# Four buffers instead of two for sorted tokens and overflow rows, and another place for the overflow units' work, in a two-expert feed-forward kernel on one Trainium2 core

## What is computed

```python
# x: (2, 2048, 512), so 4096 tokens of 512 numbers; cond: (2, 512)
ys = cond / sqrt(512)
d  = rsqrt(einsum('bi,io->bo', ys*ys, wc*wc) + 1e-8)
xf = (einsum('bsi,io->bso', x * ys[:, None, :], wc) * d[:, None, :]).reshape(4096, 512)
top1 = argmax(softmax(xf @ gate_w.T))            # one of 2 experts per token
masked = xf[None] * one_hot(top1).T[:, :, None]  # a token is zero for the other expert
h = relu(einsum('end,edh->enh', masked, w1) + b1[:, None, :])      # hidden size 2048
routing = (einsum('enh,ehd->end', h, w2) + b2[:, None, :]).sum(axis=0)
shared = relu(xf @ sw1 + sb1) @ sw2 + sb2
out = x + (routing + shared).reshape(2, 2048, 512)
```

## Time and profile before

| | |
|---|---|
| median of 3 runs | 1457.22 us (1457.13 to 1457.71) |
| the profiled execution's own time | 1471.43 us |
| its span, first to last instruction | 1469.7 us |
| mean granted clock of PE, share of full | 0.975 |
| PE busy | 1390.4 us |
| DVE, ACT, POOL busy | 904.7, 642.5, 282.6 us |
| moved by DMA | 317.65 MB, mean 216 GB/s |

### The profile page before, as it was taken

One profiled execution on the slowest core, in us unless ns is written; L12 is line 12 of the kernel. 1 busy time (PEld: TensorE's weight loads), 2 busy tenths in 40 slices (PEclk: granted clock), 3 DMA queues, 4 the chain that ended last, 5 costly groups with the idle time before them and its releaser, 6 DMA issues.

```text
span 1469.7 us, 17093 instructions
## 1 busy us (share of the span) xinstructions
PE 1390.4 (95%) x6086; PEld 1146.9 (78%) x6086; DVE 904.7 (62%) x1313; ACT 642.5 (44%) x929; POOL 282.6 (19%) x260
## 2 busy tenths in 40 slices
PE   9999999998899657999899999999999999999995
PEld 8888888887688445788788888888888887888884
DVE  7979978584796321867357787877784443333331
ACT  4455645453466332566567444444553221222220
POOL 0000006322222232200000000001001222055665
PEclk9999999999999878899999999999999999999998
DMA  6957584977998446773357797979898756366653
GB/s 211 311 181 243 193 265 163 262 249 268 302 303 258 158 155 191 258 205 109 125 187 257 247 291 247 285 249 310 289 277 297 200 148 155 90 187 165 165 128 59
DMA packets 223925, 317.65 MB, mean 216 GB/s; under 512 B 51440, under 2 KB 98544, under 8 KB 223824
## 3 DMA queue, kind: packets, MB, share of 16 engines
q1 hardware_dynamic: 200528, 267.06, 55.9%
q0 software_dynamic: 22016, 47.00, 12.9%
q10 hardware_dynamic: 1296, 2.49, 0.5%
HBM read 184.47 MB, written 140.90 MB: 221 GB/s over the span
## 4 chain that ended last, share of the span: by engine, by line
PE 84%; DMA 6%; issue 4%; POOL 2%; DVE 2%; ACT 1%; SPq 0%; ACTq 0%; POOLq 0%; DVEq 0%
PE bank L1852 38%; PE bank L1922 21%; PE bank L1951 18%; PE bank L1780 6%; DMA loose_rows<-x_rows,tab_in 3%; POOL loose_rows L847 1%; POOL out L833 1%; DMA hidden_scratch<-vb 1%; DMA rows<-sorted_scratch 1%; DMA sorted_scratch<-sorted_rows 1%; PE bank L1875 1%; DVE rows L1331 0%; DMA hidden_scratch<-vt 0%; DVE vb L1400 0%; DMA loose_rows<-loose_rows,loose_at 0%
## 5 line engine op out<-in xcount | busy, mean ns | idle before, releaser
L1852 PE MATMUL bank<-xw,w_hi 128*128 128x512 f32 x1792 | 561.3, 395 | 58.1 <-ACT vb L990 36.5
L1852 PEld LDWEIGHTS bank<-xw,w_hi 128*128 128x128 f32 x1792 | 340.8, 191 | 132.6 <-issue 34.5
L1367 DVE TENSOR_TENSOR hl<-hin,hl 128x512 fp32r<-128x512 f32 x352 | 236.5, 688 | 264.1 <-ACT hl L966 263.3
L966 ACT CAST hl<-hin 128x512 fp32r<-128x512 f32 x352 | 216.7, 621 | 385.1 <-PE bank L1951 223.6
L1852 PE MATMUL bank<-xw,w_lo 128*128 128x512 f32 x896 | 352.7, 394 | 0.0
L1951 PE MATMUL bank<-w_hi,hl 128*128 128x512 f32 x1024 | 315.9, 390 | 1.3 <-DVE res_u L1702 1.3
L1922 PE MATMUL bank<-hl,w_hi 128*128 128x512 f32 x896 | 276.0, 390 | 0.0
L1951 PEld LDWEIGHTS bank<-w_hi,hl 128*128 128x128 f32 x1024 | 192.3, 188 | 41.5 <-issue 1.7
L1951 PE MATMUL bank<-w_lo,hl 128*128 128x512 f32 x512 | 199.4, 390 | 0.0
L1852 PEld LDWEIGHTS bank<-xw,w_lo 128*128 128x128 f32 x896 | 170.8, 191 | 35.8
L1922 PEld LDWEIGHTS bank<-hl,w_hi 128*128 128x128 f32 x896 | 168.3, 188 | 34.8
(11 more groups left out here) (184 smaller groups left out, 1197.0 us busy)
## 6 DMA issues: line engine op xcount, KB each, us to landing
hin<-hidden_scratch SPq DMA_DIRECT2D x112, 512.0 KB, 4.6
hidden_scratch<-vb SPq DMA_DIRECT2D x80, 512.0 KB, 4.2
hin<-expert_hidden SPq DMA_DIRECT2D x64, 512.0 KB, 4.5
expert_hidden<-vb SPq DMA_DIRECT2D x48, 512.0 KB, 3.8
hidden_scratch<-vt SPq DMA_DIRECT2D x32, 512.0 KB, 4.4
w_new<-w_shared SPq DMA_DIRECT2D x52, 256.0 KB, 5.9
sorted_scratch<-sorted_rows POOLq DMA_DIRECT2D x48, 256.0 KB, 4.4
ring<-x_cols SPq DMA_DIRECT2D x32, 256.0 KB, 5.1
```

The lines of the kernel that those rows point to most:

```text
L966: nc.scalar.copy(hl[:, n % HL, 0, :], hin[:, n // 2 % LOADS, n % 2, :]).then_inc(hu_hi, 1)
L1367: nc.vector.tensor_tensor(hl[:, n % HL, 1, :], hin[:, n // 2 % LOADS, n % 2, :], hl[:, n % HL, 0, :].bitcast(F32), ALU.subtract).then_inc( ...
L1852: last = nc.tensor.matmul(up_bank(u, UP_BANK[c])[p][:], w[:, DOWN_W[c], pair, part], xw[:, c, x, k, :], start=(c in FRESH and n == 1), sto ...
```

## The change

Five things change.

1. `sorted_rows` has four buffers (at 208, 210, 212 and 214 KB), and POOL's loop stores tile k-2 after it has issued the gather of tile k. A gather waits for the store of tile k-4. The fourth buffer lies beyond the plan's 215 KB on tile `soft`, which is allocated right behind the plan now; `rows_u` is a view of `soft`. So ACT at the start of group 20 waits for all 48 tiles.
2. `loose_rows` has four buffers too, with the semaphores of the sort. The order of POOL's steps in the output stage stays.
3. `loose_up` uses banks 4 to 7 for products and 2 and 3 for transposes, and waits at first only for the sums of c = 3. The first transposes stand between the third and the fourth group of products; ACT's work is in the same order, and its loads of the next rows stand behind the relus. PE's last wait for all relus is gone.
4. `loose_down` runs before slot j = 8 of unit 3, uses a bank of unit 2, and PE does not wait for `loose_sum` behind it. ACT's and DVE's parts move by eight slots.
5. PE waits for `loose_down_done` before unit 4.

```diff
-LOOSE_DOWN = 3
+LOOSE_DOWN = (3, 8)
...
-        sorted_rows = [at(kb, f"sorted_rows{i}", [D]) for i, kb in enumerate((208, 210))]
+        sorted_rows = [at(kb, f"sorted_rows{i}", [D]) for i, kb in enumerate((208, 210, 212, 214))]
...
-        loose_rows = [at(kb, f"loose_rows{i}", [D]) for i, kb in enumerate((164, 166))]
+        loose_rows = [at(kb, f"loose_rows{i}", [D]) for i, kb in enumerate((164, 166, 200, 202))]
...
-        loose_banks, loose_turned = banks[0:QUADS], banks[QUADS:QUADS + 2]
+        loose_banks, loose_turned = banks[QUADS:2 * QUADS], banks[2:4]
...
             def sort_in(k):
+                i, u = k % RING, SORT[k]
                 pool.wait_ge(up_mm, PER_GROUP * SORT_GROUP + 2 * k)
-                wait(pool, sorted_out[k % 2], DMA * (k // 2))
+                wait(pool, sorted_out[i], DMA * (k // RING))
...
-            for k in range(COLS):
-                sort_in(k)
-                if k > 0:
-                    sort_out(k - 1)
-            sort_out(COLS - 1)
+            for k in range(COLS + 2):
+                if k < COLS:
+                    sort_in(k)
+                if k >= 2:
+                    sort_out(k - 2)
...
                     if u == LOOSE_UP[0] and not spilled:
-                        for i in range(2):
-                            act.wait_ge(sorted_out[i], DMA * ((SORT.index(COLS - 1) + 1) // 2))
+                        for i in range(RING):
+                            act.wait_ge(sorted_out[i], DMA * COLS // RING)
...
+                pe.wait_ge(loose_lo, 2 * x + 2)
+                pe.wait_ge(up_added, 6 * u + 2)
+                for q in range(QUADS - 1):
+                    products(q)
+                pe.wait_ge(up_added, 6 * (u + 1))
+                turn_back(0)
+                products(QUADS - 1)
+                for q in range(1, QUADS):
+                    turn_back(q)
-                pe.wait_ge(loose_relu, HC * (x + 1))
...
-                pe.wait_ge(loose_sum, 2 * x + 2)
...
+                if wide == LOOSE_DOWN[0] + 1:
+                    pe.wait_ge(loose_down_done, 2)
```

More of the change, by code:

```diff
@@ L318, in build @@
         b2_in = sem("b2_in")
-        sorted_in = [sem(f"sorted_in{i}") for i in range(2)]
-        sorted_out = [sem(f"sorted_out{i}") for i in range(2)]
+        sorted_in = [sem(f"sorted_in{i}") for i in range(RING)]
+        sorted_out = [sem(f"sorted_out{i}") for i in range(RING)]
         xr_in = [sem(f"xr_in{i}") for i in range(XR)]
@@ L577, in next_rows @@
                     tiles_done = SORT.index(W * 2 * (s + 2 - BLOCKS) - 1) + 1
-                    sp.wait_ge(sorted_out[0], DMA * (tiles_done // 2))
-                    sp.wait_ge(sorted_out[1], DMA * (tiles_done // 2))
+                    for i in range(RING):
+                        sp.wait_ge(sorted_out[i], DMA * (tiles_done // RING))
                 if s * GROUPS == LOOSE_UP[0] and q == 0:
@@ L750, in _ @@
                 sp.wait_ge(scattered[i], DMA * UNITS_E)
-            for i in range(2):
-                sp.wait_ge(loose_rows_out[i], DMA * (CAP // P // 2))
+            for i in range(RING):
+                sp.wait_ge(sorted_out[i], DMA * ((COLS + CAP // P) // RING))
         @block.gpsimd
@@ L1066, in loose_up, with flat @@
             def loose_up(e, x):
-                for q in range(QUADS):
+                def flat(q):
                     act.wait_ge(loose_clear, e + 1)
@@ L1071, in loose_up, with take @@
                     nc.scalar.copy(hq[0:S, q, :], loose_banks[q][0:S, :]).then_inc(loose_flat, 1)
-                act.wait_ge(loose_lo, 2 * x + 2)
-                loose_rows_load(x + 1)
-                for q in range(QUADS):
+                def take(q):
                     act.wait_ge(loose_back, QUADS * x + q + 1)
@@ L1079, in loose_up @@
                                              bias=b1[:, 1 + e, j:j + 1]).then_inc(loose_relu, 1)
+                for q in range(QUADS - 1):
+                    flat(q)
+                take(0)
+                flat(QUADS - 1)
+                for q in range(1, QUADS):
+                    take(q)
+                act.wait_ge(loose_lo, 2 * x + 2)
+                loose_rows_load(x + 1)
                 act.wait_ge(loose_relu, HC * (x + 1))
@@ L1695, in loose_down @@
             def loose_down(e, x):
-                bank = y_bank(LOOSE_DOWN, 0)
+                bank = y_bank(LOOSE_DOWN[0] - 1, 0)
                 dve.wait_ge(loose_y_mm, (HC + 1) * x + 1)
@@ L1863, in loose_up, with products @@
             def loose_up(u, x):
-                pe.wait_ge(loose_lo, 2 * x + 2)
-                for q in range(QUADS):
-                    if q == 0:
-                        pe.wait_ge(up_added, 6 * (u + 1))
-                        pe.wait_ge(up_kept, 8 * (u + 1))
+                def products(q):
                     pairs = slice(W * (q % 2), W * (q % 2) + W)
@@ L1877, in loose_up, with turn_back @@
                     last.then_inc(loose_mm, 1)
-                for q in range(QUADS):
+                def turn_back(q):
                     pe.wait_ge(loose_folded, QUADS * x + q + 1)
```

62 lines of the change are left out of this document (31 added, 31 removed).

## The result

| | before | after |
|---|---|---|
| median | 1457.47 us (1457.13 to 1460.28, 4 runs) | 1416.28 us (1415.08 to 1417.61, 4 runs) |
| the profiled execution's own time | 1471.43 us | 1417.61 us |
| its span | 1469.7 us | 1415.8 us |
| mean granted clock of PE | 0.975 | 0.991 |

The ratio is 0.9714, with a 95% interval of 0.9697 to 0.9730: 41 us faster. The forecast was 1402, in a range of 1386 to 1425. Between the two profiled executions 53.9 us went, of 58.6 forecast.

A forecast was written before the change was run, and what follows sets the result against it. PE, busy 1390.4 of 1469.7 us, bounds the kernel; its large gaps hang on the sort's store latency. 34.9 + 15.7 + 6.7 + 1.3 = 58.6 off 1471.4 gives 1412.8, less 11: 1402, range 1386 to 1425.

The forecast's parts named there:

- The main term: First-layer stage: faster four-buffer sort gains 34.9 us at group 20 and 15.7 at the 13.64 us gap behind it.
- the resume: PE restarting at group 20 after its wait for ScalarE and the sort: forecast at 497 us, against 531.94 before.
- the early gaps: PE's first-layer idle gaps of 4.73, 4.68, 1.24 and 0.38 us before group 20, expected to go.
- the same thing at the 8th tile: Claim that the 4.73 and 4.68 us gaps also come from SyncE waiting for late sorted tiles.
- Rival B: First-layer stores squeezed by the sort, queues splitting 347 GB/s evenly: 18 us less gain, 1420 us; chance 0.22.
- I take off 11: Final deduction, 1412.8 to 1402, for DMA stalls within the 14.2 us by which the profiled execution exceeded the median.
- the overflow unit, up: First-layer overflow unit after group 28: 3.9 us from fewer waits plus 2.8 of lower clock, 6.7 us gained.
- its next bank is wanted at 727.7 + 10.9 = 738.6, and it is free near 736, so nothing: After the first-layer overflow unit: ScalarE's later row loads would not make PE wait, costing nothing.
- Down unit, 1.3: Second-layer overflow unit, moved before j = 8 of unit 3: PE's 1.29 us gap goes, gaining 1.3 us.
- Overflow rows, nothing: Output stage: four buffers gain nothing, as GpSimd still waits for the last step's gather; some 9 us tail stays.
- Rival A: All waits vanish: gain 72.4 us, 1399 us profiled, 1387 with 12 off; chance 0.2.
- Rival C: Two sort stores land no faster than one, ScalarE waits 16 tiles more: 61 us slower, 1520 us; chance 0.04.

## Why the prediction was right, and where it was wrong

**The main term was right.** Forecast: 34.9 us at group 20 and 15.7 at the next large gap, 50.6 in all. Measured: PE finishes the work before the overflow unit at 717.44 us before and at 666.80 after, 50.6 us. The sort was to end at 494; its last store was issued at 490.4 and landed before ScalarE began its loads at 496.3. Buffers alone give 38 of the 41 us in the medians, and one store in flight gives the stall back, so the cause (a store's latency, in series with each gather) is shown from both sides.

**Its number for the resume was right by chance.** "Resume is the later of 485.4 and 494 plus the 2.8 us": PE without early gaps at 485.4, the sort at 497. The sort was ready in time, but the early gaps didn't go: 10.2 us of 11.0 stayed. The chain after has PE without a wait up to the unit:

```profile
473.27 193.54 PE bank L1859 x852
```

Of these 852 products 732 lie behind the point where PE wants c = 2 of group 20, 166.3 us at this pace, so PE got there at about 666.8 - 166.3 = 500.5 us, as late as before (500.1), and didn't wait. Not the sort set the resume, but PE itself. That is 3.5 us later than 497, and so 31.4 us were won there instead of 34.9. The other 19.2 of the 50.6 were won behind it, where 15.7 were forecast: products at the lower clock behind the two large gaps had cost some 5.6 us and not the 2.1 that were counted. With the sort done 47.6 us sooner the time is the same, which agrees.

**Why the early gaps stayed.** The forecast called them "the same thing at the 8th tile". Now SyncE asks for the first sorted rows 10 us sooner (first row before, second after):

```profile
354.78 0.33 SPq L582 DMA_DIRECT2D rows<-sorted_scratch  x1
...
344.79 0.74 SPq L580 DMA_DIRECT2D rows<-sorted_scratch  x1
```

With it the first early gap fell from 4.73 to 1.78 us; but the second went from 4.68 to 6.36. What it hangs on is the landing of one store of `hidden_scratch`, for which ScalarE waits, before (first row) as after (second row):

```profile
378.27 2.42 ACT L990 ACTIVATE vb<-bank,b 128x512 f32<-128x512 f32 x4 [8.53 <-DMA hidden_scratch<-vb]
...
377.16 2.43 ACT L989 ACTIVATE vb<-bank,b 128x512 f32<-128x512 f32 x4 [11.40 <-DMA hidden_scratch<-vb]
```

**Rival B did not happen.** Its sign was new gaps "<- hidden_scratch" between groups 11 and 19, and this gap is an old one. Nor did the queues split evenly: the hardware queue kept its share, 56.7% against 56.4%, while the software queue's rose from 23.5% to 37.1%. The Trainium skill, "DMA: Bandwidth & Descriptors", section Queues, rings and completion order, has engines take turns between queues a packet at a time. B made of this an even split of bytes, which needs packets of equal size and both queues always full; by it PE would have come 25 us late. No run shows such a delay over the whole sort; whether the rule is behind the one late store the trace doesn't tell. The same page's section Specifications gives about 358 GB/s of HBM for a core. The windows show 360 GB/s over 40 us and 353 over 30: the trace agrees over such stretches. Single slices of 5 us reach 408, and the mean over the sort, 321, stays under it.

**The first step that failed is "I take off 11".** The profiled execution of before was 14.2 us over its median, and the forecast deducted 11 of that from the time after. But an excess that sits in waits that the change removes is gone already in the sum of the profiled execution; to take it off again counts it twice. The profiled execution after is 1.3 us over its median, not 11. This is 9.7 of the 14.3 us by which 1402 was short. With nothing taken off, the forecast would have been 1412.8. That the excess of that execution sat ahead of the resume is shown against one other execution of the kernel before (6.8 of 8.4 us); for the rest it is inferred.

**The second is the overflow unit, up: 6.7 forecast, 2.0 measured.** The unit itself is shorter by the 3.9 us forecast or a little more (9.9 us, 10.3 forecast). The term failed at "its next bank is wanted at 727.7 + 10.9 = 738.6, and it is free near 736, so nothing". The products that PE can make first are those of c = 0 and c = 1, 24 of them, 5.4 us and not 10.9. The bank was wanted 5.5 us after the unit's end and came 8.8 us after it. The 2.8 us of lower clock "which I count as gone" came back as 1.8 for the same reason. This is the other 4.7 us.

**Down unit, 1.3:** the gap is gone, and the chain after runs through the unit without idle time:

```profile
1196.92 3.62 PE bank L1977 x16
1200.54 3.68 PE bank L1981 x16
1204.22 21.80 PE bank L1964 x96
```

50.6 + 2.0 + 1.3 is the whole difference of 53.9. **Overflow rows, nothing:** right, and for the reason given: the last scatter is issued 9 us behind PE's last product in both kernels, and 1.5 us behind it once the order of POOL's steps changes. The four buffers for them were not run alone.

**Rival A** (everything vanishes, 1387) fell with the early gaps. **Rival C** did not come about in the change: two stores do overlap. Its mechanism is real: 83 us of stall in the run made for it, where 31.86 + 85 = 117 were estimated, and slower than before by 2.7%.

What stays open: why the rate drops to 239 GB/s from 365 us on with busy engines, ahead of the late store. Rows, weights and stores meet there, and no run separated them. The wait for the landing of `hu` was left in place in all runs.

## What to carry to other kernels

When a transfer ring runs far below the bandwidth seen elsewhere in the trace, look at what the next gather waits for, and count how many transfers can fly; here the number of buffers decided, and the order of issue within it hardly. When a change removes waits, what a slow profiled execution lost in them must not be subtracted a second time from the sum. And for each unit that ends sooner, count how much work the next one can do before it needs a slower engine: 5 us saved at its end are nothing if the next wait begins 5 us later.

## What the runs showed of the hardware

- The same 256 KB store by the software queue, issued right behind a gather each time, landed 3.8 us after the end of its issue in the kernel before and 2.9 us after it in the run with one store in flight. There its tile had been gathered two steps ago, before one step ago; the chip was another one too. Which of these it is stays open. It is 0.9 us in each tile when nothing else runs.
- Behind a gap of 3.31 us PE fell to the lower of its clock levels (1.2 GHz) for a time: the window behind it has a granted clock of 0.66. So has the one behind the gap of 1.78 us at 364.12. The windows behind the gap of 1.24 us at 434.69, and from 500 to 510 us with PE never idle, have 1.00.

```profile
364.00:369.00 5.00, 4.88 (x14) 3.90 (x15) 4.31 (x6) 1.62 (x2) 2.12 (x2) 0.66 1.10 277
434.00:439.00 5.00, 4.31 (x19) 3.42 (x20) 5.00 (x7) 3.74 (x5) 1.55 (x2) 1.00 1.04 397
500.00:510.00 10.00, 10.00 (x45) 8.27 (x45) 5.03 (x6) 5.43 (x8) 0.00 (x0) 1.00 0.13 49
685.00:690.00 5.00, 4.52 (x13) 3.58 (x14) 1.59 (x5) 2.86 (x5) 0.00 (x0) 0.66 0.79 262
```

- The kernel before spread over 14 us in 23 runs on one chip. Kernels with the new sort spread over 2 to 9 us in 4 to 6 runs each. What the spread comes from is not shown.
